# Load order, first mixer, activation tables, last C product and stores of an early-fusion block on one core

## The reference

```python
t = conv_general_dilated(x, conv_w, window_strides=(16, 16)) + conv_b     # 64 tokens per image
q, k, v = t @ wq.T + bq, t @ wk.T + bk, t @ wv.T + bv                     # 12 heads of 16
h = softmax(q @ k.T * 16 ** -0.5) @ v @ wo.T + bo
h = concatenate([h, txt], axis=1)                                         # (16, 96, 192)

xi, res = split(layernorm(h) @ W_in, 2)                                   # 384 channels each
xc = silu(causal_depthwise_conv4(xi) + conv_b)
delta, Bm, Cm = split(xc @ W_x, [48, 64])
delta = softplus(delta @ W_dt + b_dt)
y = selective_scan(xc, delta, -exp(A_log), Bm, Cm, D_param)               # 16 states per channel
h = h + (y * silu(res)) @ W_out

up, gate = split(bitlinear(layernorm(h), w_in, g_in), 2)                  # bitlinear: RMS norm, 8-bit x,
h = h + bitlinear(silu(gate) * up, w_out, g_out)                          # ternary weights, one scale each
```

## Time and profile before

| | us |
|---|---|
| median of 3 runs (537.76 to 542.29) | 541.2 |
| the profiled execution | 541.64 |
| its span, first to last instruction | 539.8 |
| busy: DVE, PE, POOL, ACT | 399.8, 397.8, 367.3, 338.3 |
| first scan starts, last scan starts | 139.79, 500.86 |

### The profile page before, as it was taken

The page is one execution under the profiler, slowest core; times in us unless marked ns, Lnnn a source line. Parts: engine busy times, 40 slices in busy tenths (PEclk is TensorE's granted clock), DMA queues, the critical chain, the costliest instruction groups (busy, mean ns, idle before and its releaser), DMA issues.

```text
span 539.8 us, 5082 instructions
## 1 busy us (share of the span) xinstructions
PE 397.8 (74%) x1484; PEld 222.7 (41%) x1484; DVE 399.8 (74%) x481; ACT 338.3 (63%) x601; POOL 367.3 (68%) x288
## 2 busy tenths in 40 slices
PE   5929999686896585899677599875656686665753
PEld 1303677353553242565343356542323352332523
DVE  3024255622589899989999988989999989879544
ACT  1102544413967876777779857996886786796253
POOL 3002563002878988979998998998789999969401
PEclk9968999968798887999678889998987887778865
DMA  8390000005600003710000470000056100000000
GB/s 314 83 205 10 1 2 0 2 0 185 286 0 5 1 1 128 279 60 4 0 1 17 159 273 21 4 22 0 0 177 231 60 2 22 1 1 0 0 23 22
DMA packets 11547, 35.10 MB, mean 65 GB/s; under 512 B 2320, under 2 KB 6208, under 8 KB 11296
## 3 DMA queue, kind: packets, MB, share of 16 engines
q1 hardware_dynamic: 11120, 33.99, 18.7%
q10 hardware_dynamic: 400, 0.79, 0.4%
HBM read 33.40 MB, written 1.38 MB: 64 GB/s over the span
## 4 chain that ended last, share of the span: by engine, by line
POOL 31%; DVE 11%; PE 9%; issue 9%; ACT 6%; DVEq 0%; ACTq 0%; POOLq 0%
POOL big L465 15%; POOL big L471 10%; DVE PS L1305 5%; PE PS L817 4%; PE PS L593 3%; POOL big L509 2%; ACT PS L1001 2%; DVE big L1314 1%; PE PS L743 1%; DVE big L1320 1%; POOL big L447 1%; DVE big L1399 1%; ACT big L1053 1%; ACT big L1010 1%; PE PS L797 1%
## 5 line engine op out<-in xcount | busy, mean ns | idle before, releaser
L817 PE MATMUL PS<-big,eighth 128*128 128x384 f32 x384 | 170.9, 583 | 74.3 <-POOL big L471 73.2
L1305 DVE TENSOR_TENSOR_SCAN PS<-PS,big 128x768 f32<-128x768 f32 x96 | 168.6, 1756 | 18.5 <-ACT PS L1001 16.2
L465 POOL TENSOR_TENSOR big<-big,bc 128x768 f32<-128x768 f32 x96 | 175.1, 1839 | 0.0
L817 PEld LDWEIGHTS PS<-big,eighth 128*128 128x128 f32 x384 | 81.9, 224 | 144.8 <-POOL big L471 93.6
L471 POOL TENSOR_TENSOR big<-big,bc 128x768 f32<-128x768 f32 x60 | 109.5, 1824 | 37.3 <-DVE big L1314 37.1
L1001 ACT ACTIVATE PS<-big,Aneg 128x384 f32<-128x384 f32 x192 | 103.7, 572 | 39.6 <-DVE big L1320 25.4
L1010 ACT ACTIVATE big<-big,guard,Ahalf 128x380 f32<-128x380 f32 x192 | 122.5, 690 | 0.0
L1314 DVE SCALAR_TENSOR_TENSOR big<-big,PS 128x768 f32<-128x768 f32 x60 | 57.0, 951 | 5.8 <-ACT big L1010 0.5
L430 POOL TENSOR_TENSOR big<-bc,cst_sb 96x1536 f32<-96x1536 f32 x8 | 22.0, 2753 | 56.2 <-ACT bc L911 45.9
L593 PE MATMUL PS<-big,w_in_sb 96*128 96x384 f32 x96 | 42.9, 586 | 5.5 <-DVE big L1266 5.0
L593 PE MATMUL PS<-big 128*64 128x34 f32 (+3 forms) x400 | 43.8, 287 | 0.0
(11 more groups left out here) (152 smaller groups left out, 486.8 us busy)
## 6 DMA issues: line engine op xcount, KB each, us to landing
bc<-bc_rows SPq DMA_DIRECT2D x32, 768.0 KB, 4.4
bc<-in_x_cols_dram SPq DMA_DIRECT2D x3, 512.0 KB, 6.5
bc<-in_x_cols_dram SPq DMA_DIRECT2D x1, 1536.0 KB, 8.7
out_dram<-h SPq DMA_DIRECT2D x4, 288.0 KB, 2.3
big<-in_f_in_dram SPq DMA_DIRECT2D x1, 768.0 KB, 18.0
bc<-in_cw_dram ACTq DMA_DIRECT2D x1, 576.0 KB, 5.7
h<-in_bo_dram SPq DMA_DIRECT2D x3, 192.0 KB, 15.1
w_in_sb<-in_w_in_dram SPq DMA_DIRECT2D x1, 576.0 KB, 13.0
```

The source lines that it names most:

```text
L465: P.tensor_tensor(pair(vR[:, g % VRING]), part(du, q, m).unsqueeze(1).broadcast_to([128, PAIR, QT]), rows_of(g, 0), ALU.mult).then_inc(sem ...
L817: ins = pe.matmul(y_sum, eighth[:, :], vR[:, g % VRING, QT * e:QT * (e + 1)], start=False, stop=True, skip_group_check=True)
L1305: V.tensor_tensor_scan(h_, h_, vR[:, g % VRING], 0.0, ALU.mult, ALU.add).then_inc(sem("scan_done"), 1)
```

## The change

- SP issues the two FFN weights ahead of the nine bias and text loads.
- Quarter 1's pieces start at step 0 instead of -6, and all of them move within quarter 0; `FIRST_STEP` is 0.
- For quarters 2 and 3 the third convolution (`cv2`, `tu2`, `us2`), `x`, `x_out`, `dt`, `sp` and `times_u` come three steps later, `z`, `tz`, `zs` one or two, `later1` one earlier.
- Three one-column activations into a new tile `warm` make ACT load a table at another place: Softplus ahead of `x_out(0)`, Exp behind quarter 0's softplus, Silu at the last quarter's `center` step.
- In the last quarter DVE takes the C product of step 7 of each block instead of step 6.
- Each quarter is stored with two DMAs, the first two thirds behind `finish` 0, the last third behind `finish` 1.

```diff
-VECTOR_C = (1, 4, 6)
+VECTOR_C = ((1, 4, 6), (1, 4, 6), (1, 4, 6), (1, 4, 7))
...
-             dt0=-19, dt1=-19, dt2=-19, sp=-18, times_u=-16, later0=-14, later1=-11, later2=-9, edges=-6,
+             dt0=-16, dt1=-16, dt2=-16, sp=-15, times_u=-13, later0=-14, later1=-12, later2=-9, edges=-6,
...
-FIRST_MIXER = dict(stats=-6, root=-6, xn=-5, turn=-5, turned=-4, xi0=-3, xi1=-2, xi2=-2, tap0=0, tap1=0, tap2=1,
+FIRST_MIXER = dict(stats=0, root=1, xn=2, turn=2, turned=3, xi0=3, xi1=4, xi2=4, tap0=4, tap1=5, tap2=5,
...
-FIRST_STEP, LAST_STEP = -6, STEPS + 33
+FIRST_STEP, LAST_STEP = 0, STEPS + 33
...
             load("wo", wo_sb, wo)
+            load("ffn", f_in_raw, f_in.rearrange("p m n -> p (m n)"))
+            load("ffn", f_out_raw, f_out.rearrange("p m n -> p (m n)"))
...
-            load("ffn", f_in_raw, f_in.rearrange("p m n -> p (m n)"))
-            load("ffn", f_out_raw, f_out.rearrange("p m n -> p (m n)"))
             load("mix", w_in_sb[:, :, :], w_in)
...
+            def store(q, j):
+                sp.wait_ge(sem("left_f2"), ORDINAL["f2", q, j])
+                t = slice(2, 3) if j else slice(0, 2)
...
+                for q in due("center", g):
+                    if q == LAST:
+                        A.activation(warm[:, 2:3], v128[:, 0:1], ACT.Silu)
...
                 if i == 9:
+                    A.activation(warm[:, 0:1], v128[:, 0:1], ACT.Softplus)
                     x_out(0)
...
             for m in range(CT):
                 softplus(0, m)
+            A.activation(warm[:, 1:2], v128[:, 0:1], ACT.Exp)
             for g in range(FIRST_STEP, 0):
                 beside(g)
```

More of the change, by code:

```diff
@@ L60 @@
 PW = PAIR * QT
-VECTOR_C = (1, 4, 6)
+VECTOR_C = ((1, 4, 6), (1, 4, 6), (1, 4, 6), (1, 4, 7))
 MIXER = dict(stats=-32, root=-31, xn=-30, turn=-29, turned=-28, xi0=-28, xi1=-27, xi2=-27, tap0=-27, tap1=-26, tap2=-26,
-             cv0=-26, cv1=-25, cv2=-24, tu0=-25, tu1=-24, tu2=-23, us0=-24, us1=-23, us2=-22, x=-21, x_out=-20,
-             dt0=-19, dt1=-19, dt2=-19, sp=-18, times_u=-16, later0=-14, later1=-11, later2=-9, edges=-6,
-             z0=-16, z1=-15, z2=-14, tz0=-15, tz1=-14, tz2=-13, zs0=-14, zs1=-13, zs2=-12)
+             cv0=-26, cv1=-25, cv2=-21, tu0=-25, tu1=-24, tu2=-20, us0=-24, us1=-23, us2=-19, x=-18, x_out=-17,
+             dt0=-16, dt1=-16, dt2=-16, sp=-15, times_u=-13, later0=-14, later1=-12, later2=-9, edges=-6,
+             z0=-14, z1=-13, z2=-13, tz0=-13, tz1=-12, tz2=-12, zs0=-12, zs1=-11, zs2=-11)
 FFN = dict(yg0=-15, yg1=-7, yg2=1, out0=2, out1=3, add0=4, add1=5, spread=6, root_in=7, center=7, gain_in=8, max_in=10,
@@ L80 @@
 AT.update({(name, q): QSTEPS * (q + 1) + r for q in range(NQ) for name, r in FFN.items()})
-FIRST_MIXER = dict(stats=-6, root=-6, xn=-5, turn=-5, turned=-4, xi0=-3, xi1=-2, xi2=-2, tap0=0, tap1=0, tap2=1,
-                   cv0=1, cv1=2, cv2=2, tu0=2, tu1=3, tu2=3, us0=4, us1=5, us2=5, x=6, x_out=7, dt0=8, dt1=8, dt2=8, sp=9,
-                   times_u=11, later0=12, later1=14, later2=17, edges=19, z0=12, z1=13, z2=14, tz0=13, tz1=14, tz2=15,
-                   zs0=14, zs1=15, zs2=16)
+FIRST_MIXER = dict(stats=0, root=1, xn=2, turn=2, turned=3, xi0=3, xi1=4, xi2=4, tap0=4, tap1=5, tap2=5,
+                   cv0=5, cv1=6, cv2=10, tu0=6, tu1=7, tu2=11, us0=7, us1=9, us2=12, x=13, x_out=14, dt0=15, dt1=15, dt2=15, sp=16,
+                   times_u=18, later0=17, later1=18, later2=19, edges=21, z0=11, z1=12, z2=12, tz0=12, tz1=13, tz2=13,
+                   zs0=13, zs1=14, zs2=15)
 AT.update({(name, 1): g for name, g in FIRST_MIXER.items()})
@@ L194, in early_fusion @@
         bmv = sb("bmv", [128, NTL, 2])
+        warm = sb("warm", [128, 3])
         rstd = sb("rstd", [128, NTL])
@@ L297, in on_vector @@
         def on_vector(g):
-            return g % BLOCK in VECTOR_C
+            return g % BLOCK in VECTOR_C[g // QSTEPS]
         def count(vector, g):
@@ L379, in _ @@
             load("g", g_out_bc[:, :], g_out.partition_broadcast(128))
[L381 to L384, removed]
+            def store(q, j):
+                sp.wait_ge(sem("left_f2"), ORDINAL["f2", q, j])
+                t = slice(2, 3) if j else slice(0, 2)
+                sp.dma_start(out[QB * q:QB * (q + 1)].rearrange("b l d -> (b l) d").rearrange("(i p) d -> p i d", p=128)[:, t],
+                             tiles(q, t)).then_inc(sem("out_stored"), 16)
             def rows(q):
@@ L400, in _ @@
                 if q >= 2:
[L401 to L404, removed]
+                    store(q - 2, 0)
+                    store(q - 2, 1)
+            for q in range(NQ - 2, NQ):
+                store(q, 0)
+                store(q, 1)
+            sp.wait_ge(sem("out_stored"), 32 * NQ)
         @block.gpsimd
```

## The result

The changed kernel takes 514.0 us (median of 4 runs, 513.84 to 515.47) against 540.92 for the kernel before in the same session (537.76 to 542.29): a ratio of 0.9516, 95% interval 0.9471 to 0.9561. Forecast were 519.4 and 512 to 528. The profiled execution took 515.47 with a span of 513.7, so 26.1 of the 539.8 are gone: 19.7 ahead of the first scan, 5.4 from there to the end of the last gate, 1.0 behind it.

What follows compares the result with a forecast made beforehand. Bounds: a chain of engines at front and end, nearly full DVE and POOL in the loop. 13.4 + 6.0 − 1.2 + 1.4 + 1.9 + 0.3 = 21.8 saved, giving 519.4 against the median 541.2; own range 515 to 524, eight-in-ten 512 to 528.

Steps and rivals of the forecast that it cites:

- Loads, 13.4: Front: FFN weights landing by 21 remove PE's 10.7 hole before QKV and 2.7 of slow clock, 13.4 us saved.
- Front to loop, 6.0: Third softplus to first scan: quarter 1's pieces no longer stand between, first decay ends at 133.8 against 139.79, 6.0 saved.
- Statistics, −1.2: Quarter 0 of the loop: DVE's moved pieces, 0.88 + 0.31, come back there and are paid in full, 1.2 lost.
- the rival in which the loop takes the second hole back: Quarter 0: waits eat what the earlier first scan gave, terms 6.0 − 1.2 + 1.4 become zero, 525.6 us; chance 0.15.
- Rest of the loop, 1.4: Loop: waits of 1.98 (ACT's tanh) and 2.03 (quarter 0's FFN) go, half of times_u twice costs 2.65; 1.4 saved.
- the loop gaining more: Rival in the loop: 4.0 and half of the other 6.8 of waits go, 7.4 instead of 1.4, 513.4 us; chance 0.16.
- Last C product, 1.9: End of the last quarter: C product ends at 503.7 on DVE instead of 505.55 on POOL, PE and gate follow, 1.9 saved.
- the forecast's sign: Sign at the loop's end: the last gate comes 1.9 earlier after the last scan.
- Tables at the end 0, store 0.3: End: earlier Silu table gives nothing since DVE's product waits for PE; last store, shrunk to a third, saves 0.3.
- The rival that had the weights landing late: Front: 5.1 of the wait for FFN weights and 2.7 of slow clock remain, 527.2 us; chance 0.07.
- The late mixer: Rival at the starts of quarters 1 to 3: next quarter's mixer comes too late and DVE stands; 554 at s = 5; chance 0.04.
- The sign of DVE's idle time: Sign in the loop: DVE idle about 27 from first scan to last gate (30.3 − 1.4 − 1.9).

Runs made afterwards that it cites:

- the control: The changed kernel once more, unedited, on a third chip beside three kernels with added PE matmuls: 517.03 us, ratio 0.9549 to the kernel before.
- the first mixer alone: The kernel before with only quarter 1's mixer begun at step 0 instead of -6 (FIRST_MIXER and FIRST_STEP): 532.22 us, ratio 0.9876.
- the old table in the changed kernel: The changed kernel with the earlier MIXER table of steps for quarters 2 and 3 put back: 518.13 us, ratio 0.9637 to the kernel before.

## Why the forecast held, and where it was off

*Loads, 13.4:* measured 13.6, and confirmed alone. The 21 taken for the landing was slightly late: the reductions began at 19.7 and ended at 22.9, so the weights had landed by 19.7 (by 21.1 in the control). The price of the issues was wrong too, since each held SP for 0.5, not 3.7; it made no difference because DVE had 6.15 to spare. The same issue takes 3.7 behind nine small loads and 0.5 ahead of them, so the earlier trace rows told of its place in the queue. The loads pushed back were waited for by nobody on this chain.

*Front to loop, 6.0:* measured 6.06, of which 5.80 come with the start at step 0 and 0.25 with the Exp line. No drain appears behind the table load, neither with the one-column activation (118.92 follows 117.62 + 1.28) nor without it (118.19 follows 116.89 + 1.28). Nor does one stand ahead of it (the softplus ends at 117.02 + 0.58, the load begins at 117.62). In the 14 profiles of this study the next activation starts 0.01 behind the load at 217 of 224 loads, and at the other seven ACT waits for PE. So the gain is the 6.0 of the row, not the 4.6 that the Trainium skill's page "ScalarE: Activation LUTs", section "What ACT_TABLE_LOAD costs", would have given with its drain.

*Statistics, −1.2:* they stand in the loop with 0.88 + 0.31, paid as forecast. Quarter 0 grew from 88.1 to 89.8, so the rival in which the loop takes the second hole back fell.

*Rest of the loop, 1.4:* this is the term that was mis-sized. By it and the two beside it (−1.2 and 1.9) the stretch from first scan to last gate was to shrink by 2.1; it shrank by 5.4 in the profiled execution, which makes the term 4.7. Three steps of it failed. The half of `times_u` that was charged twice, 2.65, was not seen: scans wait 2.3 for POOL in both kernels. Waits of scans for ACT fell by 4.5, where I had named only the 1.98, and most of that comes with the first mixer's spreading, as the run with it alone shows. Against that, DVE's `later` scans cost 3.1 more, which no term had. What I had called the loop gaining more (4.0 and half of 6.8, with a chance of 0.16) is what the waits did: of the 9.3 of idle time that went, 1.88 are the last gate's, and the other 7.4 are that rival's number. The term ended at 4.7 only because part was paid back in slower scans. The 2.03 was gone after the change, but its removal alone was no gain in time.

How much of the 4.7 belongs to the change is open. By the control's 365.6 the term is 1.7, near the forecast's 1.4. In the nine profiles with the first mixer's new start and the one or the other table the loop takes 362.6 (four), 365.3 to 366.1 (four, the first mixer alone among them) or 369.2 (the old table in the changed kernel), against 367.4 to 368.0 in the three with the loop unedited; what sets one execution apart from another here no run shows.

*Last C product, 1.9:* the gate's wait fell by 1.88, and 1.74 came off from step 94's scan to the gate's end. Counted from the last scan, as the forecast's sign has it, it is only 0.88 (6.90 to 6.02): the other 0.95 lies ahead of that scan, which no longer has a C product before it. The working had this right and the sign did not.

*Tables at the end 0, store 0.3:* the last store landed sooner, and the time from the last `finish` to the end of the span fell from 2.7 to 2.4: 0.3, in every profile with the split stores. The other 0.7 of the tail's gain is luck: it lies in the same PE instructions at another clock, among them f_out's last matmuls with 2.10 before and 1.48 now, and the run with the first mixer alone, which has no edit there, shows it as well (31.05 from the last gate to the end, where it was 32.08).

The rival that had the weights landing late fell with DVE's 6.15 of waiting. The late mixer fell too: no scan of the loop waits longer for ACT than the first one, 2.51.

From the profiled execution the forecast was 519.8; it took 515.5. The 4.3 between them are 3.3 in the loop, 0.7 behind the gate and 0.2 in the loads. The median of 514.0 lies below the forecast's own range, 515 to 524, and beside the 513.4 of the rival in which the loop gains more; only the wider range holds it. The control on the third chip, 517.0 with a ratio of 0.955, lies nearer to the forecast's 519.4 of 541.2 (0.960). The sign of DVE's idle time was off as well, 21.0 (22.6 in the control) where about 27 was forecast.

## What to carry to other kernels

In a chain of engines, look for the queue that a late load stands in before pricing its bytes: two lines moved were worth half of the gain. In a loop with one nearly full engine, count that engine's waits by releaser and its busy time by instruction separately; a small net change can be two large ones. And where PE waits a few microseconds on a critical chain, look at the granted clock of the stretch behind the wait: matmuls for nobody, which end before the wait does, gave back 8.0 here.

## What the runs showed of the hardware

- **The clock behind short waits.** In the control, a wait of 3.9 of PE in attention and two of 4.3 and 6.1 in the tail were followed by a granted clock of 0.50 (95 to 100), 0.55 (495 to 500) and 0.57 (505 to 510), that is mostly 1.2 GHz, and keeping PE busy in them gave 4.7 and 3.4. The mean clock differs between executions of one kernel: in the first two batches the 20 runs of the kernel before took 538.0 to 543.0 at mean clocks of 0.853 to 0.866, or 533.7 to 536.3 at 0.872 to 0.881. (On the third chip one run of 536.35 had 0.860, so the clock is not all of it.) That is as large as the effect of a whole part of this change.
- **DVE's scan beside POOL.** The `later` scan, 128x384 with both inputs in SBUF, takes 0.92 by itself (116.70, above) and 2.28 at 129.74, where POOL is 0.35 into an operation of its own:

```profile
129.39 1.81 POOL L470 TENSOR_TENSOR big<-big,bc 128x768 f32<-128x768 f32 x1
```

  Over the twelve the mean is 1.51 before and 1.77 after, up to 2.90. The Trainium skill, "SBUF — State Buffer", section "Who interferes with whom", says that a VectorE instruction with two SBUF inputs contends with a GpSimd instruction that reads SBUF, that the shared port pair is an exclusive lock, and that the order of issue decides who blocks. The traces agree: 129.39 + 1.81 is 131.20, and the scan ends 0.82 after that. It is the rule in all 14 profiles: of their 168 `later` scans 151 start while a `TENSOR_TENSOR` of POOL is running, and each of them ends 0.81 to 0.88 after that operation, whether it takes 0.92 in all or 2.90; the other 17 take 0.92 or 0.93. So the 3.1 are time in which scans stand behind POOL's operations. No run moved those away, so whether the kernel would be 3.1 faster without them is not shown.
